# Windowed attention on Trainium2: where the band's mask for the row maxima is added

## The chip, the cores and the metric

One core of a Trainium2 chip (trn2) runs the whole program in one launch. The metric is the device time of that launch in microseconds. The kernel before takes 2782.56 us (median of three runs, 2774.63 to 2786.53).

## The reference, cut to what matters

The program is four layers of a transformer on 1024 tokens of 256 features, each layer an attention and a feed-forward part. The change concerns only the second attention (layer 1): 32 query heads and 8 key heads of 64 features, with rotary positions and a sink, a number per head that takes part in the softmax. Its core, cut:

```python
attn = jnp.einsum('bqhmd,bkhd->bhmqk', q, k) * sm_scale
...
mask = (q_pos >= k_pos) & (q_pos < k_pos + SW)
attn = jnp.where(mask, -jnp.inf, attn)
...
w = jax.nn.softmax(jnp.concatenate([attn, sink], axis=-1), axis=-1)[..., :-1]
out = jnp.einsum('bhmqk,bkhd->bqhmd', w, v).reshape(B, L, NQ * HD)
return out @ W_out
```

With SW = 64 a query leaves out itself and the 63 keys before it, and attends to all others of the 1024. In the kernel the left-out positions get -1e30 before the softmax: for a block of 128 queries they lie in a band of 192 columns of keys.

What the kernel's softmax needs before the exponentials is an upper bound of each row's scores, the row maximum. It is computed ahead, from a shorter product of queries and keys, and the mask must be in those scores too.

## The kernel before, in words

**Stages.** `layer1_attention` runs a norm, a projection (`project`, lines near 900 to 1110), `attend_window` (L1533) and an output product. Only `attend_window` changes, and what it is given in `masks_dram`.

**Batches.** `attend_window` works on 16 batches of two heads (`PER` = 2). Each has 16 tiles of scores (8 blocks of 128 keys, 2 halves of 512 queries) for each of the two heads. For batch n TensorE makes the scores (L1831, L1832, and a mask product L1834, which stays), ScalarE the exponentials (L1951), GpSimd the sums over the blocks of keys (L1754, 28 adds per batch), and TensorE the products with the values (L1847). A loop over j = 0 to 7 does two key blocks of both heads at each step.

**Maxima of the next batch, in between.** While batch n is in that loop, TensorE computes the scores for the maxima of batch n + 1, in a query-by-key orientation: 16 segments, each of one block qb of 128 queries by one half s of the keys (512), for two heads: two products of 64 rows, side by side (L1774), into a pair of banks (128 x 1024 elements). VectorE reduces each pair to its maximum in one instruction (`maxima`, L2017: 2 x 512 to 2 elements, a1h_mseg). Nine of the 16 segments are banded: the band of masked keys falls in them, 64, 128 or 192 columns of each head. Segments with their numbers, (qb, s): 0 (0,1); 1 (0,0) banded, 128 columns; 2 (4,0) banded, 64; 3 (1,1); 4 (1,0) banded, 192; 5 (4,1) banded, 128; 6 (2,1); 7 (2,0); 8 (3,1); 9 (3,0); 10 (5,0); 11 (5,1); 12 (6,0); 13 (6,1); 14 (7,0); 15 (7,1); of 7 to 15 the odd ones are banded, 192.

In the loop these go by visits: 0 and 1, then 2 (step j = 0); 3 and 4, then 5 (j = 1); 6 and 7 (j = 2); 8 and 9; 10 and 11; 12 and 13; 14 and 15 (j = 3 to 6). A visit computes the products of its segments and then, in the banded one, the mask: `mask_maxima` adds, for each 64 columns and each head, a small product (L1796) of `mk_rows` (0, 1 and -1 in bfloat16) by a triangle of -1e30, 2 to 6 products a visit. The last of them raises `a_ready`, for which VectorE waits.

**The ring of two.** The segments' products, and five other things, go in turn through two pairs of banks (`ring`, `wait_spare`), in the order in which they are issued: segments 0 to 5, D, 6, 7, T, 8 to 11, R, 12 to 15, M. M (L1807) carries the batch's row maxima over to the other orientation, D (L1859) the sums of exponentials over keys, T (L1869) their transposes, R (L1878) the inverses spread over rows. Each waits until the one two places before it has been read: D for the read of segment 4, T for that of segment 6, segment 8 for that of 7.

**VectorE's order** is written out: per step j its maxima; at j = 1 after segment 5 the low parts of the next queries (`queries_low`, L1704, two instructions, SBUF only); at j = 2 the inverse (L2055, L2058) after segment 7; at j = 4 the scaling (L2064); at j = 7 the maximum of the two segments of a block (L2030) and with the sink (L2033, both SBUF only), for which M waits, then the spread maxima (L2042), and in two of four batches the next keys (L2005 a cast, L2007 a subtraction). An engine works its instructions off in that order.

**The first batch** has no batch before it: its segments run in visits (0, 1), (3, 4), (6, 7), (8, 9) before everything else, then M, and the other eight within steps 0 and 1, and the row maxima of its second half of queries at step 2.

The lines that set what a segment costs on either engine:

```python
ps = spare(("A", n, k))
for a in range(PER):
    mm = pe.matmul(ps[:, a, :], ..., kn[HI[a], G % 2, a, half(s)], start=True, stop=lo >= hi, ...)
...
dve.tensor_reduce(mseg[:, :, qb, s], spare(("A", n, k))[:, :, :], AX.X, ALU.max).then_inc(a_read, 1)
```

Of the kernel before, what the change touches and what calls it, by code (L numbers as in the profile page):

```python
# [1532 lines left out]
def attend_window(nc, core, name, qk, k_dram, v, scale, groups, spread_dram, masks_dram, sink, before, sync, gpsimd):  # L1533
# [54 lines left out]
    with ExitStack() as ctx:  # L1588
        sem = lambda n: nc.alloc_semaphore(f"{name}_{n}")
        sb = lambda n, shape, dt=F32: ctx.enter_context(nc.sbuf_tensor(f"{name}_{n}", shape, dt))  # L1590
        c_in, kn_in, prep, keys_out = sem("c_in"), sem("kn_in"), sem("prep"), sem("keys_out")
        k0_in, k1_ones = (sem("k0_in0"), sem("k0_in1")), sem("k1_ones")
# [7 lines left out]
        mk_rows = sb("mk_rows", [P, 3 * P + 64], BF16)  # L1600
# [8 lines left out]
        mk_rows_raw = stage[:, 1, 0:3 * P + 64]  # L1609
# [6 lines left out]
        def first_in(sp, written):  # L1616
            sp.dma_start(mk_raw[:, :, :], masks_dram[:, 0:2 * MW].rearrange("p (u m) -> p u m", u=2)).then_inc(c_in, 16)
            sp.dma_start(mk_rows_raw, masks_dram[:, 2 * MW:2 * MW + 3 * P + 64]).then_inc(c_in, 16)
# [14 lines left out]
        def constants(pool, written):  # L1633
            pool.wait_ge(c_in, 64)
            pool.tensor_scalar(mk[:, :, :], mk_raw[:, :, :], 1.0, None, ALU.mult).then_inc(prep, 1)
            pool.tensor_scalar(mk_rows[:, :], mk_rows_raw, 1.0, None, ALU.mult).then_inc(prep, 1)
            pool.memset(mpos[:, :, :].bitcast(F32), 0.0).then_inc(prep, 1)
            pool.tensor_scalar(sk8[:, :], sk[:, :], 1.0 / scale, None, ALU.mult).then_inc(prep, 1)
            pool.tensor_scalar(nident[:, :], core.ident[:, :], -1.0, None, ALU.mult).then_inc(prep, 1)
# [28 lines left out]
        def spare(key):  # L1668

            return ring[use[key] % 2]  # L1670

# [87 lines left out]
        def _(pe):  # L1759
            def maxima(n, k):  # L1760
# [11 lines left out]
                lo, hi = masked(k)  # L1772
                for a in range(PER):
                    mm = pe.matmul(ps[:, a, :], QA[n % 2][HI[a], a, qb * P:(qb + 1) * P],  # L1774
                                   kn[HI[a], G % 2, a, half(s)], start=True, stop=lo >= hi, tile_position=(64 * a, 0))
                if lo >= hi:
                    mm.then_inc(a_ready, 1)

            def masked(k):

                qb, s = SEGS[k]
                return max((qb + 1) * P - BAND, s * HALF), min((qb + 1) * P, (s + 1) * HALF)

            def mask_maxima(n, k):

                qb, s = SEGS[k]
                lo, hi = masked(k)
                if lo >= hi:
                    return
                ps = spare(("A", n, k))  # L1790
                for c in range((lo - (qb + 1) * P + BAND) // 64, 3):
                    c0 = (qb + 1) * P - BAND + 64 * c
                    if c0 >= hi:
                        continue
                    for a in range(PER):
                        mm = pe.matmul(ps[:, a, c0 - s * HALF:c0 - s * HALF + 64], mk_rows[HI[a], c * P:(c + 1) * P],  # L1796
                                       mk_rows[HI[a], 3 * P:3 * P + 64], start=False, stop=c0 + 64 == hi,
                                       tile_position=(64 * a, 0))
                mm.then_inc(a_ready, 1)
# [82 lines left out]
            def visit(n, ks):  # L1882
# [3 lines left out]
                for k in ks:  # L1886
                    mask_maxima(n, k)
# [110 lines left out]
        def _(dve):  # L1998
# [15 lines left out]
            def maxima(n, k):  # L2014
                qb, s = SEGS[k]
                dve.wait_ge(a_ready, use["A", n, k] + 1)
                dve.tensor_reduce(mseg[:, :, qb, s], spare(("A", n, k))[:, :, :], AX.X, ALU.max).then_inc(a_read, 1)  # L2017
# [1382 lines left out]
def lay_out(inp):  # L3400
# [28 lines left out]
    bands = np.zeros((64, 3 * P + 64), np.float32)  # L3429
    i, j = np.arange(64), np.arange(64)[None, :]  # L3430
    for b in range(2):
        own, nxt = P * b + 64 * b, P * (b + 1) + 64 * b
        bands[i[1:], own + i[:-1]] = 1.0
        bands[i[1:], nxt + i[:-1]] = -1.0
        bands[0, nxt:nxt + 64] = 1.0
    bands[:, 3 * P:][j >= i[:, None]] = -1e30
    a["window"] = np.concatenate([m.reshape(P, 4 * P), np.concatenate([bands, bands])], 1)
# [109 lines left out]
```

## Time and profile before

| | |
|---|---|
| median of three runs | 2782.56 us |
| the profiled execution | 2789.25 us |
| its span on the chip | 2787.5 us |
| mean granted TensorE clock | 0.928 |
| TensorE busy (matmul) | 2531.3 us, 91% |
| VectorE busy | 1627.8 us, 58% |
| ScalarE busy | 1259.5 us, 45% |
| GpSimd busy | 1289.6 us, 46% |
| second attention | about 626 to 1340 us of the span |

The page of the profile calls the engines PE (matmuls), PEld (weight loads), DVE (VectorE), ACT (ScalarE), POOL (GpSimd) and SP (SyncE). A row of a timeline is: start in us from the span's start, length in us (of xN instructions merged: from the first start to the last end), engine, line, operation, output <- inputs, shapes, and in brackets how long the engine sat idle before and what released it. Matmuls overlap in their rows, so costs on TensorE are read from one start to the next. The granted clock is 1.00 at 2.4 GHz and 0.50 at 1.2 GHz.

### The profile page before, as it was taken

The numbers are of one execution on the slowest core, as the hardware profiler recorded it, in microseconds if no ns is written. First come the engines' busy times: TensorE is split into PE (matmuls) and PEld (weight loads), VectorE is DVE, ScalarE is ACT, GpSimd is POOL, SyncE is SP. The second block draws the span as 40 slices with busy tenths as digits, with TensorE's granted clock in tenths as the row PEclk, the third lists the DMA queues.
The fourth block names the chain that finished last, engine by engine and source line by source line (L and its number), as shares of the span: only waits on it lengthen the run. The fifth ranks groups of instructions, "written<-read, shape, count | busy, mean of one in ns | idle before, by whom it ended". The sixth has DMA issues, their size and how long they took to land. (4 is left out here: it accounts for less than half of the span.)

```text
span 2787.5 us, 40697 instructions
## 1 busy us (share of the span) xinstructions
PE 2531.3 (91%) x14471; PEld 1686.6 (61%) x14474; DVE 1627.8 (58%) x2168; ACT 1259.5 (45%) x2174; POOL 1289.6 (46%) x1130
## 2 busy tenths in 40 slices
PE   6887999878999999999878888789999989998798
PEld 4444777654444444444664446578888867776676
DVE  4663555577666766664436633477767745554555
ACT  4464333464555555555334552256555543333222
POOL 4100344486888888888521003254545523442243
PEclk9798999898999999999976979899999998998799
DMA  1000111121101101010000001100100001110111
GB/s 58 1 2 15 35 46 48 44 79 38 39 16 38 39 24 38 16 35 1 27 24 1 1 1 49 52 22 20 31 20 20 21 10 41 45 45 15 30 42 41
DMA packets 39709, 81.63 MB, mean 29 GB/s; under 512 B 7552, under 2 KB 21120, under 8 KB 39040
## 3 DMA queue, kind: packets, MB, share of 16 engines
q1 hardware_dynamic: 39264, 79.41, 10.2%
q8 instruction: 98, 1.61, 0.3%
q14 instruction: 59, 0.48, 0.1%
q10 hardware_dynamic: 288, 0.13, 0.0%
HBM read 59.07 MB, written 2.62 MB: 22 GB/s over the span
## 5 line engine op out<-in xcount | busy, mean ns | idle before, releaser
L2017 DVE TENSOR_REDUCE a1h_mseg<-bank 128x2 f32<-128x1024 f32 x256 | 302.7, 1222 | 187.3 <-PE bank L1774 173.4
L63 POOL TENSOR_TENSOR f_wh<-f_raw,ones_r 128x768 fp32r<-128x768 f32 (+1 forms) x74 | 111.8, 1511 | 545.6 <-PE bank L464 367.2
L1951 ACT ACTIVATE a1h_prob<-bank 128x512 f32<-128x512 f32 x366 | 206.1, 598 | 165.8 <-PE bank L1834 83.8
L1754 POOL TENSOR_TENSOR a_qk<-a_qk,a1h_prob 128x512 f32<-128x512 f32 x186 | 238.7, 1315 | 50.8 <-ACT a1h_prob L1951 50.8
L453 PE MATMUL bank<-x_norm_h,f_wh 128*128 128x512 f32 x592 | 244.2, 412 | 6.5 <-PEq L3247 2.5
L453 PE MATMUL bank<-x_norm_l,f_wh 128*128 128x512 f32 x592 | 238.7, 403 | 0.0
L453 PE MATMUL bank<-x_norm_h,f_wl 128*128 128x512 f32 x592 | 237.5, 401 | 0.0
L656 DVE SCALAR_TENSOR_TENSOR f_tf<-bank,f_bias,f_sg 128x512 f32<-128x512 f32 x148 | 111.0, 751 | 191.8 <-PE bank L453 185.4
L1832 PE MATMUL bank<-a1h_ql,a1h_k 128*128 128x512 f32 x512 | 203.2, 397 | 0.0
L544 ACT ACTIVATE f_hhi<-f_hf 128x512 fp32r<-128x512 f32 x124 | 78.3, 632 | 276.3 <-DVE f_hf L664 276.3
L1847 PE MATMUL bank<-a1h_prob,a_v 128*64 128x512 f32 x732 | 179.8, 604 | 0.0
L670 DVE TENSOR_TENSOR f_hlo<-f_hf,f_hhi 128x512 fp32r<-128x512 f32 x124 | 116.1, 938 | 82.7 <-ACT f_hhi L544 82.4
L533 ACT ACTIVATE f_sg<-bank,f_bias 128x512 f32<-128x512 f32 x148 | 101.9, 688 | 130.1 <-PE bank L453 130.1
L453 PEld LDWEIGHTS bank<-x_norm_h,f_wh 128*128 128x128 f32 x592 | 114.0, 192 | 50.8 <-issue 24.3
L453 PEld LDWEIGHTS bank<-x_norm_l,f_wh 128*128 128x128 f32 x592 | 114.1, 193 | 28.2
L364 POOL TENSOR_TENSOR f_wl<-f_raw,f_wh 128x768 fp32r<-128x768 f32 (+1 forms) x74 | 127.8, 1727 | 5.9
L453 PEld LDWEIGHTS bank<-x_norm_h,f_wl 128*128 128x128 f32 x592 | 114.7, 194 | 25.5
L464 PE MATMUL bank<-f_hhi,f_wh 128*128 128x512 f32 x296 | 118.5, 400 | 12.8 <-DVE f_hlo L670 12.8
L1831 PE MATMUL bank<-x_norm_h,a1h_kn 128*128 128x512 f32 x256 | 120.4, 470 | 4.7 <-DVE a1h_k L2012 3.4
L2871 POOL TENSOR_TENSOR l2a_rope<-l2a_rope,l2a_tab 128x512 f32<-128x512 f32 x64 | 81.2, 1276 | 88.9 <-ACT l2a_rope L2736 87.8
L1754 POOL TENSOR_TENSOR x_norm<-x_norm,a1h_prob 128x512 f32<-128x512 f32 x86 | 112.3, 1338 | 20.6 <-ACT a1h_prob L1951 20.6
L1455 ACT ACTIVATE a2h_prob<-bank 128x512 f32<-128x512 f32 (+3 forms) x192 | 83.7, 488 | 81.2 <-PE bank L1285 56.9
(595 smaller groups left out, 6337.8 us busy)
## 6 DMA issues: line engine op xcount, KB each, us to landing
f_raw<-in_l_w_dram SPq DMA_DIRECT2D x66, 385.0 KB, 3.1
a1h_st_q<-a_qk SPq DMA_DIRECT2D x128, 128.0 KB, 2.4
l2a_qkraw<-in_l2a_wqk_dram SPq DMA_DIRECT2D x32, 128.0 KB, 2.1
l2a_vraw<-in_l2a_wvg_dram SPq DMA_DIRECT2D x8, 512.0 KB, 3.8
f_raw<-in_l_w_dram SPq DMA_DIRECT2D x8, 449.0 KB, 3.3
a_qk<-l_keys SPq DMA_DIRECT2D x24, 128.0 KB, 2.8
a1p_raw<-in_l1a_w_dram SPq DMA_DIRECT2D x20, 128.0 KB, 2.1
a_qk<-in_l1a_wo_dram SPq DMA_DIRECT2D x16, 128.0 KB, 2.1
```

The lines of the kernel that those rows point to most:

```text
L63: return pool.tensor_tensor(dst, src, one.to_broadcast(list(src.shape)), ALU.mult)
L364: pool.tensor_tensor(wl[:, slot, :], raw[:, slot, 0:B], wh[:, slot, :].bitcast(F32), ALU.subtract).then_inc(w_split, 1)
L453: mm = pe.matmul(out[:, :], w[:, slot, c0:c0 + P], x, start=n == 0, stop=n == 3 * n_k - 1)
L464: mm = pe.matmul(acc[m][h][:, :], w[:, slot, c0:c0 + P], x[:, h, :], start=begin and n == 0, stop=False, skip_group_check=True)
L656: dve.scalar_tensor_tensor(tf[:, h, :], up[h][:, :], bias[:, slot, 1:2], sg[:, h, :], ALU.add, ALU.mult).then_inc(t_ready, 1)
L670: dve.tensor_tensor(hl[:, h, :], src[:, h, :], hh[:, h, :].bitcast(F32), ALU.subtract).then_inc(hl_ready, 1)
L1754: pool.tensor_tensor(out, first, slot_of[t % NP], ALU.add).then_inc(sum_done, 1)
L1831: pe.matmul(bank[:, :], kn[:, G % 2, a, keys], QA[n % 2][:, a, half(h)], start=True, stop=False)
L1832: mm = pe.matmul(bank[:, :], k1[:, a, keys], ql[:, n % 2, a, half(h)], start=False, stop=lo >= hi)
L1847: pe.matmul(core.bank[5][64 * a:64 * a + 64, :], v[:, kb, 2 * (n // 4) + a, :], slot_of[t % NP], start=kb == 0, stop=kb == TB - 1, skip_gr ...
L1951: act.activation(slot_of[t % NP], core.bank[2 + t % 3][:, :], ACT.Exp, scale=scale).then_inc(p_ready, 1)
L2017: dve.tensor_reduce(mseg[:, :, qb, s], spare(("A", n, k))[:, :, :], AX.X, ALU.max).then_inc(a_read, 1)
```

## The change

The nine banded segments of each batch get their mask from VectorE. It adds the rows of `mk` (bfloat16, the mask in query-by-key orientation, already in SBUF; its half `mk[:, 1]` was loaded before too, without a reader; L1834 reads the other) to the banded columns of both heads, in place in the bank pair: 2 x 64, 2 x 128 or 2 x 192 elements a partition, one `tensor_tensor` with one operand and the output in PSUM and the other operand in SBUF. It waits for it (`band_added`) and reduces as before. The 46 mask products per batch go, and with them `mask_maxima`, the tile `mk_rows`, its DMA and its conversion by GpSimd. `a_ready` is now raised by the segment's own product. Nothing else is moved.

```diff
--- before.py
+++ after.py
@@ -1589,6 +1589,7 @@
         sem = lambda n: nc.alloc_semaphore(f"{name}_{n}")
         sb = lambda n, shape, dt=F32: ctx.enter_context(nc.sbuf_tensor(f"{name}_{n}", shape, dt))
         c_in, kn_in, prep, keys_out = sem("c_in"), sem("kn_in"), sem("prep"), sem("keys_out")
+        band_added = sem("band_added")
         k0_in, k1_ones = (sem("k0_in0"), sem("k0_in1")), sem("k1_ones")
         q_in = [sem("q_in0"), sem("q_in1")]
         q_hi, q_lo, kn_steps, k1_act, k1_dve = sem("q_hi"), sem("q_lo"), sem("kn_steps"), sem("k1_act"), sem("k1_dve")
@@ -1597,7 +1598,6 @@
         ou_done, on_done, den_copied, r_steps, rx_done = sem("ou"), sem("on"), sem("den_copied"), sem("r_steps"), sem("rx")
         spread = sb("spread", [P, TB])
         mk = sb("mk", [P, 2, MW], BF16)
-        mk_rows = sb("mk_rows", [P, 3 * P + 64], BF16)
         nident = sb("nident", [P, P])
         mpos = sb("mpos", [P, PER, 64], F32R)
         sk = sb("sk", [P, BATCHES * PER])
@@ -1606,7 +1606,6 @@
         kn = sb("kn", [P, 2, PER, T], F32R)
         stage = sb("stage", [P, 2, HALF])
         mk_raw = stage[:, 0, 0:2 * MW].rearrange("p (u m) -> p u m", u=2)
-        mk_rows_raw = stage[:, 1, 0:3 * P + 64]
 
         def load_queries(sp, n, a):
             for r in range(4):
@@ -1615,7 +1614,6 @@
 
         def first_in(sp, written):
             sp.dma_start(mk_raw[:, :, :], masks_dram[:, 0:2 * MW].rearrange("p (u m) -> p u m", u=2)).then_inc(c_in, 16)
-            sp.dma_start(mk_rows_raw, masks_dram[:, 2 * MW:2 * MW + 3 * P + 64]).then_inc(c_in, 16)
             sp.dma_start(spread[:, :], spread_dram).then_inc(c_in, 16)
             sp.dma_start(sk[:, :], sink.partition_broadcast(P)).then_inc(c_in, 16)
             written(sp, 0)
@@ -1631,9 +1629,8 @@
                 sp.dma_start(k_dram[G], qk[:, NQ + G, :]).then_inc(keys_out, 16)
 
         def constants(pool, written):
-            pool.wait_ge(c_in, 64)
+            pool.wait_ge(c_in, 48)
             pool.tensor_scalar(mk[:, :, :], mk_raw[:, :, :], 1.0, None, ALU.mult).then_inc(prep, 1)
-            pool.tensor_scalar(mk_rows[:, :], mk_rows_raw, 1.0, None, ALU.mult).then_inc(prep, 1)
             pool.memset(mpos[:, :, :].bitcast(F32), 0.0).then_inc(prep, 1)
             pool.tensor_scalar(sk8[:, :], sk[:, :], 1.0 / scale, None, ALU.mult).then_inc(prep, 1)
             pool.tensor_scalar(nident[:, :], core.ident[:, :], -1.0, None, ALU.mult).then_inc(prep, 1)
@@ -1669,6 +1666,17 @@
 
             return ring[use[key] % 2]
 
+        def masked(k):
+
+            qb, s = SEGS[k]
+            return max((qb + 1) * P - BAND, s * HALF), min((qb + 1) * P, (s + 1) * HALF)
+
+        def bands_added(n, k):
+
+            if n == 0:
+                return sum(SEGS[x] in BANDED for x in FIRST[:FIRST.index(k) + 1])
+            return n * len(BANDED) + sum(SEGS[x] in BANDED for x in range(k + 1))
+
         def reads(n, k):
 
             return n * len(SEGS) + (k if n else FIRST.index(k)) + 1
@@ -1769,33 +1777,9 @@
                         pe.wait_ge(kn_steps, G * 4 + 4)
                 wait_spare(pe, ("A", n, k))
                 ps = spare(("A", n, k))
-                lo, hi = masked(k)
                 for a in range(PER):
                     mm = pe.matmul(ps[:, a, :], QA[n % 2][HI[a], a, qb * P:(qb + 1) * P],
-                                   kn[HI[a], G % 2, a, half(s)], start=True, stop=lo >= hi, tile_position=(64 * a, 0))
-                if lo >= hi:
-                    mm.then_inc(a_ready, 1)
-
-            def masked(k):
-
-                qb, s = SEGS[k]
-                return max((qb + 1) * P - BAND, s * HALF), min((qb + 1) * P, (s + 1) * HALF)
-
-            def mask_maxima(n, k):
-
-                qb, s = SEGS[k]
-                lo, hi = masked(k)
-                if lo >= hi:
-                    return
-                ps = spare(("A", n, k))
-                for c in range((lo - (qb + 1) * P + BAND) // 64, 3):
-                    c0 = (qb + 1) * P - BAND + 64 * c
-                    if c0 >= hi:
-                        continue
-                    for a in range(PER):
-                        mm = pe.matmul(ps[:, a, c0 - s * HALF:c0 - s * HALF + 64], mk_rows[HI[a], c * P:(c + 1) * P],
-                                       mk_rows[HI[a], 3 * P:3 * P + 64], start=False, stop=c0 + 64 == hi,
-                                       tile_position=(64 * a, 0))
+                                   kn[HI[a], G % 2, a, half(s)], start=True, stop=True, tile_position=(64 * a, 0))
                 mm.then_inc(a_ready, 1)
 
             def max_rows(n, kind="M"):
@@ -1883,8 +1867,6 @@
 
                 for k in ks:
                     maxima(n, k)
-                for k in ks:
-                    mask_maxima(n, k)
 
             for ks in HEAD:
                 visit(0, ks)
@@ -2014,6 +1996,12 @@
             def maxima(n, k):
                 qb, s = SEGS[k]
                 dve.wait_ge(a_ready, use["A", n, k] + 1)
+                lo, hi = masked(k)
+                if lo < hi:
+                    part = spare(("A", n, k))[:, :, lo - s * HALF:hi - s * HALF]
+                    band = mk[:, 1, lo - (qb - 1) * P:hi - (qb - 1) * P].unsqueeze(1)
+                    dve.tensor_tensor(part, part, band.to_broadcast([P, PER, hi - lo]), ALU.add).then_inc(band_added, 1)
+                    dve.wait_ge(band_added, bands_added(n, k))
                 dve.tensor_reduce(mseg[:, :, qb, s], spare(("A", n, k))[:, :, :], AX.X, ALU.max).then_inc(a_read, 1)
 
             def blocks(n, kind):
@@ -3426,15 +3414,7 @@
     c2 = np.arange(2 * P)[None, :]
     m[:, 0][(c2 >= k) & (c2 < k + 64)] = -1e30
     m[:, 1][(P + k - c2 >= 0) & (P + k - c2 < 64)] = -1e30
-    bands = np.zeros((64, 3 * P + 64), np.float32)
-    i, j = np.arange(64), np.arange(64)[None, :]
-    for b in range(2):
-        own, nxt = P * b + 64 * b, P * (b + 1) + 64 * b
-        bands[i[1:], own + i[:-1]] = 1.0
-        bands[i[1:], nxt + i[:-1]] = -1.0
-        bands[0, nxt:nxt + 64] = 1.0
-    bands[:, 3 * P:][j >= i[:, None]] = -1e30
-    a["window"] = np.concatenate([m.reshape(P, 4 * P), np.concatenate([bands, bands])], 1)
+    a["window"] = m.reshape(P, 4 * P)
     pos = np.arange(T, dtype=np.float32)
 
     r = np.arange(P)
```

## Rows read from the trace of the kernel before

**Rows 1.** Busy time by stretch: start:end, length, then busy us of each engine, clock, DMA.
```profile
640.00:660.00 20.00, 16.62 (x80) 8.27 (x79) 12.01 (x12) 6.35 (x12) 8.39 (x7) 0.75 0.09 20
820.00:860.00 40.00, 37.32 (x224) 17.84 (x222) 25.76 (x23) 20.81 (x35) 30.85 (x25) 1.00 0.17 40
```

**Rows 2.** Timeline of TensorE: two visits, one of two segments, one of one (start, length).
```profile
929.16 0.74 PE L1774 MATMUL bank<-a1h_kn,x_norm_l 64*128 64x512 f32 x4
929.74 0.26 PE L1796 MATMUL bank<-a1h_mk_rows 64*128 64x64 bf16 x6
929.93 0.65 PE L1847 MATMUL bank<-a1h_prob,a_v 128*64 128x512 f32 x2
...
964.07 0.50 PE L1774 MATMUL bank<-a1h_kn,x_norm_h 64*128 64x512 f32 x2
964.41 0.23 PE L1796 MATMUL bank<-a1h_mk_rows 64*128 64x64 bf16 x4
964.57 1.06 PE L1859 MATMUL bank<-a_qk,ones_r 128*32 128x512 f32 x8
```

**Rows 3.** Single lines, VectorE: duration in ns, least/median/most.
```profile
L1089 DVE TENSOR_TENSOR bank<-bank,a1p_tab x40: 689/699/700, 541.9 to 609.5; 128x512 f32<-128x512 f32 x40
...
L2064 DVE TENSOR_TENSOR a_qk<-a_qk,bank x16: 1220/1222/1223, 719.3 to 1347.4; 128x1024 f32<-128x1024 f32 x16
```

**Rows 4.** Timeline, first stretch, in two batches; last row: waits (us, times, longest).
```profile
917.20 0.73 PE L1774 MATMUL bank<-a1h_kn,x_norm_l 64*128 64x512 f32 x4
917.74 2.36 DVE L2017 TENSOR_REDUCE a1h_mseg<-bank 128x2 f32<-128x1024 f32 x2 [1.70 <-PE bank L1774]
920.34 0.62 PE L1859 MATMUL bank<-a_qk,ones_r 128*32 128x512 f32 x1
921.71 3.59 DVE L1704 TENSOR_TENSOR a1h_ql<-a1h_st_q,x_norm_l 64x1024 fp32r<-64x1024 f32 x2
922.92 7.21 POOL L1754 TENSOR_TENSOR a_qk<-a_qk,a1h_prob 128x512 f32<-128x512 f32 x5 [1.58 <-ACT a1h_prob L1951]
926.62 0.66 PE L1869 MATMUL bank<-ident,a1h_dsum 128*128 128x128 f32 x4 [0.42 <-DVE a1h_mseg L2017]
...
961.43 0.73 PE L1774 MATMUL bank<-a1h_kn,x_norm_h 64*128 64x512 f32 x4
965.83 2.46 DVE L1704 TENSOR_TENSOR a1h_ql<-a1h_st_q,x_norm_h 64x1024 fp32r<-64x1024 f32 x2
970.36 0.66 PE L1869 MATMUL bank<-ident,a1h_dsum 128*128 128x128 f32 x4
...
PE bank L1869 <- DVE a1h_mseg L2017: 2.0, 5, 0.4
```

**Rows 5.** Timeline, second stretch: GpSimd, VectorE and TensorE around the row maxima.
```profile
939.01 9.93 POOL L1754 TENSOR_TENSOR a_qk<-a_qk,a1h_prob 128x512 f32<-128x512 f32 x8 [2.14 <-ACT a1h_prob L1951]
947.74 1.23 DVE L2030 TENSOR_TENSOR a1h_mrow<-a1h_mseg 128x16 f32<-128x16 f32 x1
949.00 0.18 DVE L2033 TENSOR_TENSOR a1h_mpos<-a1h_mrow,a1h_sk 128x16 fp32r<-128x16 f32 x1
949.13 2.51 POOL L1754 TENSOR_TENSOR a_qk<-a_qk,a1h_prob 128x512 f32<-128x512 f32 x2 [0.20 <-ACT a1h_prob L1951]
949.96 0.44 PE L1807 MATMUL bank<-a1h_nident,a1h_mpos 128*64 128x128 f32 x4
```

**Rows 6.** Single lines, VectorE: one subtraction behind a cast, beside GpSimd and without.
```profile
L2007 DVE TENSOR_TENSOR a1h_kn<-a_qk,a1h_kn x6: 2189/2194/2197, 735.1 to 1128.0; 64x1024 fp32r<-64x1024 f32 x6
...
L1647 DVE TENSOR_TENSOR a1h_kn<-x_norm,a1h_kn x2: 1218/1220/1223, 612.3 to 614.6; 64x1024 fp32r<-64x1024 f32 x2
```

**Rows 7.** Timeline, the start of the second attention.
```profile
626.40 9.53 DVE L2017 TENSOR_REDUCE a1h_mseg<-bank 128x2 f32<-128x1024 f32 x8 [2.06 <-PE bank L1774]
658.27 0.17 DVE L2030 TENSOR_TENSOR a1h_mrow<-a1h_mseg 128x8 f32<-128x8 f32 x1
659.07 1.28 POOL L1754 TENSOR_TENSOR a_qk<-a_qk,a1h_prob 128x512 f32<-128x512 f32 x1 [5.55 <-ACT a1h_prob L1951]
```

## The prediction

> **What bounds the kernel now.** I read the busy time by stretch first. In the second attention (about 626 to 1340 us) TensorE is busy 37 of 40 us or more at the full granted clock, the stretch shown being the least busy of the steady ones, VectorE about 26; only the first 20 us or so differ, with the clock at 0.75 [rows 1]. So TensorE is the bound on average, and a mask taken off it looks like a gain. The page and the waits do not say whether VectorE, which gets the work, is late at the few places where TensorE asks it for a result. For that I read one batch of two heads in order of time (a batch is 43 to 45 us; a batch's maxima are taken in nine visits, each of which ends with one masked segment).
>
> **The products removed.** A batch has 23 blocks of 64 masked columns, for two heads: 46 products, 736 in all, and all go. Their busy times overlap, so I take starts. A visit of two segments has its first mask product 0.58 us after its first product, a visit of one 0.34: a pair of products costs 0.24, and the step into the masks 0.10. The six masks and the step out of them take 0.19 (929.74 to 929.93), four take 0.16 [rows 2]. Per visit that is 0.29 with six and 0.26 with four (a few have two). Part of it stays, since the next work sits in another tile form anyway: between nothing and the 0.10 seen on the way in. I take 0.07, nearer the row. A visit gives 0.22 (six masks) or about 0.20 (four or two), bounds 0.16 to 0.29; nine visits, 1.9 us a batch.
> The Trainium skill (TensorEngine Tiling (Array Packing), Tiling Modes) states that changing the tiling mode drains TensorE; the masks use the same form as the products before them, so by that rule the drain stays and only the lower end of the saving comes, 0.03 less a visit, and the sum would be about 2 us higher. No row shows a step out without masks.
>
> **The adds.** No row shows this add, but one is almost it: VectorE's multiply in place on a bank, 512 elements, 0.689 to 0.700 us, of which I take 0.695. One of 1,024 with a bank and a tile in SBUF takes 1.222 [rows 3]. The slope is 1.03 ns an element, so 384 elements cost 0.56, 256 cost 0.43, 128 cost 0.30. The reduction waits for the add: 0.03 us more, as between the two small operations at 947.74 and 949.00 [rows 5]. Per batch 6 x 0.59 + 2 x 0.46 + 0.33 = 4.8 us of VectorE. Bounds: 0.30 an add (half the price; then the first collision below goes too) and 0.70 (the 512-element row whole). I take the line through the two rows, since both are of this form.
>
> **Stretch 1, from the visit of segments 3 and 4 to the transposes of the sums (L1869).** Before, it takes 9.42 us (917.20 to 926.62) in five batches, where the transposes wait for VectorE 0.4 us, and 8.93 (961.43 to 970.36) in the nine others [rows 4]. They need the bank that segment 6 was read from; VectorE reads it after segments 3, 4, 5 and the two halves of the queries' low part (L1704). After: first reduction 0.54 behind the visit, 1.18, add 0.59, 1.18, add 0.46, 1.22, then L1704. The sums over keys (L1859) need segment 4's bank, which is read at 0.54 + 1.18 + 0.59 + 1.22 + 0.07 = 3.60, where TensorE would have been there at 3.14 - 0.42 = 2.72: a stall of 0.88. GpSimd's next add comes 2.58 behind L1859 (920.34 to 922.92), at 6.18. L1704's first half then runs from 5.20 to 6.42, so GpSimd waits in it and comes before its second half.
> That collision is real in the trace: in the five long batches GpSimd starts (922.92) just as the first half ends, and the pair takes 3.59 in place of 2.46. And a GpSimd that waits gets in between two VectorE instructions 0.03 apart: the subtraction behind the cast takes 2.19 in all six cases, 1.22 where it meets no GpSimd add [rows 6]. So: 5.20 + 1.22 + 1.25 + 1.25 + 1.22 + 0.07 = 10.21. That is 0.79 more than before in five batches, 1.28 in nine.
>
> **Stretch 2, from there to the row maxima's product (L1807).** 23.34 us (926.62 to 949.96). Four visits give 0.88. But VectorE's maximum of two segments (L2030) asks at 947.74, while GpSimd's eighth add in a run is on (939.01 to 948.94), and ends with it at 948.97; GpSimd's ninth comes at 949.13 only, so L2033 slips in [rows 5]. After, L2030 asks 0.37 later (0.59 for the last add, less 0.22 for the visit before), still inside the eighth add, and ends as before. The ninth is ready 0.44 earlier, 948.69, so GpSimd is waiting when L2030 ends and goes first: L2033 ends at about 950.4 and L1807 starts at 950.5, 0.54 late rather than 0.44 early. The two visits further up still give 0.44. Net +0.10.
>
> **Stretch 3, to the next visit of segments 3 and 4.** Two visits: -0.37. The adds there (0.46 + 0.33) end before anyone asks.
>
> **The start.** The first eight reductions run without a gap, 9.53 us, and scores wait for them: four adds, 2.2 us. The first batch's other eight go through the two banks in two groups, with TensorE behind them: about 0.6 a group. Then the row maxima of its second half: L2030 asks at 658.27, just ahead of GpSimd's run at 659.07 [rows 7]. After, four more adds (2.3) stand before it, against 1.2 by which GpSimd's run moves, so it and L2033 land in the run and wait as in stretch 2: about 1.9 more for TensorE. Total +5.3; what the visits of this batch save is in it, since TensorE stands waiting there.
>
> **The rest.** One of SyncE's DMAs for constants and one GpSimd conversion go, both in the projection before; nothing that TensorE or VectorE waits for there comes from them, so I take nothing, with a gain of a microsecond or two as the other end. SyncE's loads of the next queries wait for L1704, so they start up to 2 us later; ScalarE asks for them half a batch later, so they stay covered.
>
> **Sum.** Five batches at +0.79 + 0.10 - 0.37 = 0.52, nine at 1.01: 11.7. With the start 17.0 us. The profiled execution took 2789.25 (span 2787.5), which gives 2806; it stands 6.7 above the median of 2782.56, and against that the forecast is 2800. What this measurement can tell from no change is about 0.5%, 14 us, so the forecast lies just outside.
>
> **Rivals.**
> First, faster: VectorE's adds are covered, both collisions stay away. It is decided at 6.42, the end of L1704's first half: if GpSimd asks later (now 0.24 before), or if a waiting GpSimd loses to the next VectorE instruction. Then stretch 1 is TensorE's, 8.93 - 0.64 + 0.88 = 9.17, stretch 2 gives 0.88: nine batches at -1.01, five at -1.50, and the start at 3.4: -13, 2769. For it: VectorE has a third of its time free. Against it: six cases of six. The Trainium skill (SBUF — State Buffer, A bandwidth-pool intuition that's wrong) has a blocked GpSimd start about 115 ns after VectorE's end; by it VectorE's next instruction would come first, and the time would be this one. Chance 0.09.
> Second, one collision of the two: without the second, a batch gives back 0.98 us and the start 1.9: 17.0 - 15.6 = +1.4; without the first, nine batches at -0.03, five at -0.52, and the start's 5.3: +2.4. Time 2784 to 2785, chance 0.28. What speaks for it is how thin the margins are: 0.24 us for the first, 0.28 for the second (948.69 against 948.97).
> Third, dearer: the adds cost 0.70, or TensorE's new stalls of about 1 us bring the granted clock down, as in the start, where it was 0.75. Against it: all steady stretches show 1.00, that with the most idle time (2.7 of 40 us) too [rows 1]. The adds alone make the way to the transposes 0.14 + 0.27 longer in fourteen batches, and the start 1.1: 7 us, 2807; the clock more, 2812 and up. Chance 0.08.
> The forecast itself has 0.55, of which a fifth falls under 14 us (a saving near 0.29).
>
> **How the numbers follow.** Faster by over 0.5%: 0.09. Within: 0.28 + 0.11 = 0.39. Slower: 0.44 + 0.08 = 0.52. The range leaves out the lower part of the first rival and the clock: 2774 to 2811. The forecast's own range is 2793 to 2807 (saving per visit 0.16 to 0.30, adds 0.50 to 0.65).
>
> **What would show it.** Right: L1859 with a wait for VectorE near 0.9 us, L1869 near 1 us, in nearly all batches; L1704's second halves at 2.4 us; L2033 at 1.4 and not 0.18; the adds at 0.56; a batch of 44 to 45.5 us; the granted clock 1.00. Wrong: L1704 pairs at 2.46 and L2033 at 0.18 (first rival), adds far from 0.56, visits whose next work starts less than 0.5 or more than 0.6 us behind their first product (six masks).

## The result, and the profile after

| | before | after |
|---|---|---|
| median of nine runs each | 2786.68 us | 2797.70 us |
| ratio, 95% interval | | 1.0043 [1.0029, 1.0057] |
| span of the profiled execution | 2787.5 us | 2800.6 us |
| TensorE busy, instructions | 2531.3 us, 14471 | 2518.0 us, 13735 |
| VectorE busy, instructions | 1627.8 us, 2168 | 1713.4 us, 2312 |

The kernel became 11 us slower, where 17 had been forecast. That is a little less than the 0.5% (14 us) that the prediction set as the line of what can be told, so it falls in the class "within", which had 0.39, and not in "slower", which had 0.52; with nine runs a side the interval lies above 1 all the same. The forecast time of 2800 us lies 2.3 us from the measured 2797.70, closer than the change itself (17 for 11), only because the median of the kernel before is 2786.68 over nine runs and was 2782.56 over three: that part is luck.

Where the time went is read more finely in the trace than in the run times. I call **stage** the time from the second attention's first product of maxima to its last sums over keys (L1859, now L1843). It is 715.1 us before (625.85 to 1340.94) and 728.4 after (628.70 to 1357.12): +13.3. The rest of the span is 2072.4 and 2072.2. Over all twelve kernels of this study that rest lies between 2065.8 and 2076.0, so a single span, or a median of few runs, scatters by some us with nothing that the edits touch; a batch of the stage repeats within 0.05 us in most cases. The stage has three parts in each batch, the prediction's stretches: from the visit of segments 3 and 4 to the transposes of the sums (L1869, now L1853); from there to the row maxima's product (L1807, now L1791); from there to the next visit.

The first stretch in the trace of after, a batch at the same point of the stage as in [rows 4], TensorE, VectorE and GpSimd merged (start, length, engine, line):
```profile
927.39 0.73 PE L1781 MATMUL bank<-a1h_kn,x_norm_l 64*128 64x512 f32 x4
927.93 1.23 DVE L2005 TENSOR_REDUCE a1h_mseg<-bank 128x2 f32<-128x1024 f32 x1 [0.71 <-PE bank L1781]
928.05 1.08 PE L1831 MATMUL bank<-a1h_prob,a_v 128*64 128x512 f32 x4
929.08 0.56 DVE L2003 TENSOR_TENSOR bank<-bank,a1h_mk 128x384 f32<-128x384 f32 x1
929.66 1.23 DVE L2005 TENSOR_REDUCE a1h_mseg<-bank 128x2 f32<-128x1024 f32 x1
...
930.80 0.42 DVE L2003 TENSOR_TENSOR bank<-bank,a1h_mk 128x256 f32<-128x256 f32 x1
930.95 0.62 PE L1843 MATMUL bank<-a_qk,ones_r 128*32 128x512 f32 x1 [0.53 <-DVE a1h_mseg L2005]
931.26 1.23 DVE L2005 TENSOR_REDUCE a1h_mseg<-bank 128x2 f32<-128x1024 f32 x1
932.40 3.50 DVE L1712 TENSOR_TENSOR a1h_ql<-a1h_st_q,x_norm_l 64x1024 fp32r<-64x1024 f32 x2
933.53 10.93 POOL L1762 TENSOR_TENSOR a_qk<-a_qk,a1h_prob 128x512 f32<-128x512 f32 x8 [1.97 <-ACT a1h_prob L1933]
935.93 1.23 DVE L2005 TENSOR_REDUCE a1h_mseg<-bank 128x2 f32<-128x1024 f32 x1
937.21 0.66 PE L1853 MATMUL bank<-ident,a1h_dsum 128*128 128x128 f32 x4 [0.52 <-DVE a1h_mseg L2005]
```
What to see: the add costs 0.56 us and the reduction follows some 0.03 later; the sums over keys now wait 0.53 for VectorE; GpSimd's add starts as the first half of the low part ends and stands before the second (the pair takes 3.50); the transposes wait 0.52. From 927.39 to 937.21 it is 9.82 us, and 9.81 to 9.83 in all fourteen batches, where it was 8.9 in nine and 9.4 in five.

The low part's line in the after trace, the two halves of every second batch (ns, least/median/most):
```profile
L1712 DVE TENSOR_TENSOR a1h_ql<-a1h_st_q,x_norm_h x14: 1206/1727/2267, 711.5 to 1244.2; 64x1024 fp32r<-64x1024 f32 x14
```
The halves are 1.21 and 2.27 us; with every pair at 3.49 or 3.50, that is one of each in every batch.

The end of the second stretch in the same batch:
```profile
949.41 12.43 POOL L1762 TENSOR_TENSOR a_qk<-a_qk,a1h_prob 128x512 f32<-128x512 f32 x10 [2.05 <-ACT a1h_prob L1933]
956.76 0.56 DVE L2003 TENSOR_TENSOR bank<-bank,a1h_mk 128x384 f32<-128x384 f32 x1
957.35 1.23 DVE L2005 TENSOR_REDUCE a1h_mseg<-bank 128x2 f32<-128x1024 f32 x1
958.62 0.79 DVE L2018 TENSOR_TENSOR a1h_mrow<-a1h_mseg 128x16 f32<-128x16 f32 x1
959.43 1.20 DVE L2021 TENSOR_TENSOR a1h_mpos<-a1h_mrow,a1h_sk 128x16 fp32r<-128x16 f32 x1
960.78 0.44 PE L1791 MATMUL bank<-a1h_nident,a1h_mpos 128*64 128x128 f32 x4 [0.60 <-DVE a1h_mpos L2021]
```
GpSimd's run no longer has a gap behind its eighth add (ten in a row, against eight and two in [rows 5]), so the second small step waits for an add too: 1.20 and not 0.18. The stretch is 23.57, against 23.34.

TensorE's waits in the after trace, 690 to 1330 us (total us, times, longest). Before, the first and third were not there and the second was 2.0, 5 times [rows 4]:
```profile
PE bank L1791 <- DVE a1h_mpos L2021: 8.9, 15, 0.6
PE bank L1853 <- DVE a1h_mseg L2005: 7.2, 14, 0.5
PE bank L1843 <- DVE a1h_mseg L2005: 7.2, 14, 0.5
```

The stretches of [rows 1] in the trace of after: the clock of the steady part stays 1.00, VectorE is at 30.5 of 40 us where it was about 26.
```profile
640.00:660.00 20.00, 12.99 (x44) 6.65 (x44) 11.51 (x16) 7.12 (x10) 7.48 (x6) 0.67 0.00 1
820.00:860.00 40.00, 36.87 (x179) 16.66 (x178) 30.46 (x32) 21.32 (x37) 32.77 (x26) 1.00 0.17 40
```

What a visit gained, TensorE in the after trace, a visit of two segments and one of one:
```profile
972.12 0.74 PE L1781 MATMUL bank<-a1h_kn,x_norm_h 64*128 64x512 f32 x4
972.78 1.08 PE L1831 MATMUL bank<-a1h_stage,a_v 128*64 128x512 f32 x4
...
969.19 0.50 PE L1781 MATMUL bank<-a1h_kn,x_norm_h 64*128 64x512 f32 x2
969.62 0.50 PE L1815 MATMUL bank<-x_norm_l,a1h_kn 128*128 128x512 f32 x1
```
The next work starts 0.66 us behind the first product, against 0.77 in [rows 2]. So six masks with the step into them were worth 0.11 us, not 0.22. The visit of one segment shown here is that of segment 2, which had two masks: 0.43, where it is 0.48 in the trace before. Four masks in segment 5's visit, the one in [rows 2], were worth 0.09: e1, where nothing waits there, has 0.42 in place of 0.50 to 0.51. Four in segments 0 and 1 gave 0.08. Over nine visits that is 0.9 us a batch.

### The profile page after: what moved, and what is told of

Same layout as the page of the kernel before. It is cut to its first block and busy times, and to the rows that moved or that the text cites. A ratio compares the mean times of both kernels' runs of the same rounds, so it can differ in the third digit from the quotient of the medians.

```text
span 2800.6 us, 39367 instructions
## 1 busy us (share of the span) xinstructions
PE 2518.0 (90%) x13735; PEld 1669.2 (60%) x13738; DVE 1713.4 (61%) x2312; ACT 1259.5 (45%) x2174; POOL 1287.8 (46%) x1129
## 5 line engine op out<-in xcount | busy, mean ns | idle before, releaser
L2005 DVE TENSOR_REDUCE a1h_mseg<-bank 128x2 f32<-128x1024 f32 x256 | 313.2, 1226 | 133.9 <-PE bank L1781 128.4
L364 POOL TENSOR_TENSOR f_wl<-f_raw,f_wh 128x768 fp32r<-128x768 f32 (+1 forms) x74 | 128.0, 1730 | 5.9
L1815 PE MATMUL bank<-x_norm_l,a1h_kn 128*128 128x512 f32 x256 | 118.7, 464 | 0.8
## 6 DMA issues: line engine op xcount, KB each, us to landing
a1h_st_q<-a_qk SPq DMA_DIRECT2D x128, 128.0 KB, 2.4
l2a_qkraw<-in_l2a_wqk_dram SPq DMA_DIRECT2D x32, 128.0 KB, 2.3
a_qk<-l_keys SPq DMA_DIRECT2D x24, 128.0 KB, 2.6
a1p_raw<-in_l1a_w_dram SPq DMA_DIRECT2D x20, 128.0 KB, 2.0
a_qk<-in_l1a_wo_dram SPq DMA_DIRECT2D x16, 128.0 KB, 2.0
```

The costliest lines, as they stand in the source:

```text
L364: pool.tensor_tensor(wl[:, slot, :], raw[:, slot, 0:B], wh[:, slot, :].bitcast(F32), ALU.subtract).then_inc(w_split, 1)
L1815: pe.matmul(bank[:, :], kn[:, G % 2, a, keys], QA[n % 2][:, a, half(h)], start=True, stop=False)
```

## The experiments

All parts are in us and from one profiled execution each. The code shown is part of the difference to the kernel before, for e1 and e5 of that to the kernel after. Start: first product to the first visit of segments 3 and 4; 13: the thirteen batches from there, with their sums of the three stretches; the ratio is to the kernel before on the same chip.

| kernel | ratio, 95% | stage | start | 13 | to T | T to M | M on |
|---|---|---|---|---|---|---|---|
| before | | 715.1 | 73.4 | 567.3 | 118.5 | 303.7 | 145.2 |
| after | 1.0043 [1.0029, 1.0057] | 728.4 | 77.8 | 575.2 | 127.7 | 306.1 | 141.4 |
| e1 neither | 0.9981 [0.9968, 0.9995] | 708.8 | 72.6 | 561.9 | 115.8 | 304.8 | 141.4 |
| e2 both | 1.0056 [1.0038, 1.0075] | 731.3 | 80.2 | 575.9 | 127.3 | 303.6 | 145.0 |
| e3 after, low part moved | 1.0053 [1.0034, 1.0072] | 729.8 | 80.6 | 574.5 | 120.0 | 303.6 | 150.9 |
| e4 before, low part moved | 1.0013 [1.0000, 1.0026] | 720.9 | 74.7 | 571.6 | 116.1 | 306.5 | 149.0 |
| e5 after, one step | 1.0016 [0.9998, 1.0034] | 720.7 | 77.3 | 568.6 | 127.7 | 297.4 | 143.5 |
| e6 products for segments 4, 5 | 1.0006 [0.9987, 1.0026] | 714.3 | 76.7 | 563.2 | 114.8 | 306.8 | 141.6 |
| e7 products in the first batch | 1.0060 [1.0037, 1.0084] | 724.8 | 73.9 | 575.3 | 127.2 | 306.5 | 141.7 |
| e8 before, adds for 4, 5 | 1.0025 [1.0010, 1.0040] | 725.1 | 73.2 | 576.6 | 128.0 | 303.7 | 145.0 |
| e9 combined | 0.9954 [0.9939, 0.9969] | 705.2 | 74.5 | 556.8 | 115.0 | 298.2 | 143.7 |
| e10 before, one step | 1.0002 [0.9986, 1.0019] | 715.1 | 73.4 | 567.3 | 118.5 | 303.7 | 145.1 |

**e1, neither products nor adds.** What the products alone are worth. It is the kernel after without the add and its wait, so the maxima hold no mask at all.
```diff
-                lo, hi = masked(k)
-                if lo < hi:
...
-                    dve.tensor_tensor(part, part, band.to_broadcast([P, PER, hi - lo]), ALU.add).then_inc(band_added, 1)
```


> The changed kernel without its adds: no mask in the maxima at all (that part of the computation is left out: the band's -1e30 in the maxima). It shows what the products alone are worth. Theory (the after trace: a visit's next work starts 0.66 us behind its first product, before 0.77, so a visit is worth 0.11 and not 0.22; the rest of the change is what VectorE's adds cost): nine visits give 1.0 us a batch; the way to the transposes may take back 0.3 of it where GpSimd now meets the low part of the queries. 6 to 14 us below before, 2773 to 2780, ratio 0.995 to 0.998; VectorE busy as before. Rival (the products are worth the forecast's 1.9 us a batch and the adds cost that much more): 27 us below before, 2760, ratio 0.990. Rival (the loss does not come from the adds at all, but from the products' absence, the clock or the order): within 3 us of after, 2795 and up.

Measured: 2779.76 against 2783.83 us, ratio 0.9981, stage 6.3 below before. The low end of the theory was 6; the first rival's 27 is out, and so is the second's time near that of after. The visits give 0.11 each, but the stretch from transposes to row maxima is 23.54 in place of 23.36 in eleven of thirteen batches, although its four visits are 0.44 shorter. In the other two of the thirteen it is 22.9; there the first of VectorE's two steps meets no GpSimd add (0.18 us). The two steps in the e1 trace, 690 to 1400 us (ns), and one instance:
```profile
L2015 DVE TENSOR_TENSOR a1h_mpos<-a1h_mrow,a1h_sk x15: 1153/1202/1303, 690.8 to 1295.4; 128x16 fp32r<-128x16 f32 x15
...
948.81 1.34 DVE L2012 TENSOR_TENSOR a1h_mrow<-a1h_mseg 128x16 f32<-128x16 f32 x1
950.18 1.23 DVE L2015 TENSOR_TENSOR a1h_mpos<-a1h_mrow,a1h_sk 128x16 fp32r<-128x16 f32 x1
```
So the second collision needs no adds. Taking the products away is enough: TensorE's scores, and GpSimd's adds behind them, come earlier, and the gap in GpSimd's run closes.

**e2, products and adds both.** What the adds alone cost.
```diff
                 dve.wait_ge(a_ready, use["A", n, k] + 1)
+                lo, hi = masked(k)
+                if lo < hi:
...
+                    dve.tensor_tensor(part, part, band.to_broadcast([P, PER, hi - lo]), ALU.add).then_inc(band_added, 1)
```


> The kernel before with its mask products kept and VectorE's adds put in as well (the mask is added twice, which changes no weight). It shows what the adds alone cost. Theory: the way to the transposes is VectorE's, 9.82 us as in the after trace, 0.41 more than before in five batches and 0.89 more in nine; the row maxima come about 0.6 late; the start costs 4.4 + 1: 5 x 1.0 + 9 x 1.5 + 5.4 = 24 us above before, 2810, that is 11 to 13 above after. Rival (a visit's products are worth the forecast's 0.22): 0.22 x 9 x 14 = 27 above after, 2825. Rival (VectorE's adds are what costs, and the products' time is hidden under them): equal to after within 3 us, 2798.

Measured: 2803.31 us, ratio 1.0056; stage 16.2 above before, where 24 was expected, and 2.9 above after, where 11 to 13 was: a miss on both. What came, at its edge, is the last rival, by which the products' time is hidden under the adds (within 3 us of after). The second small step, 690 to 1400 us, is not held up here:
```profile
L2046 DVE TENSOR_TENSOR a1h_mpos<-a1h_mrow,a1h_sk x15: 174/176/178, 699.1 to 1318.7; 128x16 fp32r<-128x16 f32 x15
```
So with the products kept, the adds cost nothing in the second stretch (303.6): TensorE isn't waiting for VectorE there. They cost it in the first stretch (+8.8) and at the start (+6.8). With the adds in, dropping the products is worth 2.9 us in the whole stage, and the thirteen batches only 0.7: the first stretch is VectorE's anyway, the second becomes 2.5 us longer and the third 3.6 shorter.

**e3 and e4, the low part moved.** L1712 taken out of the first stretch.
```diff
-                    if n + 1 < BATCHES and j == 1:
-                        for a in range(PER):
-                            queries_low(dve, n + 1, a)
...
+                    if n + 1 < BATCHES and j in (3, 4):
+                        queries_low(dve, n + 1, j - 3)
```


> The changed kernel with the low part of the next queries taken out of VectorE's way to the transposes: its first half behind the maxima of the fourth pair of tiles, its second behind the scaling in the fifth, where VectorE has 1.2 to 1.7 us free. Theory (VectorE's order with the low part in it, held up by a GpSimd add, sets when the transposes start): their wait for VectorE goes, 9.82 becomes 9.2 to 9.3 (the sums over keys still wait 0.5), 14 x 0.55 = 8 us below after, 2790, ratio to before 1.001. Rival (the time lost is in the adds before the sums over keys and before the row maxima, and what is won here is waited for there): within 2 us of after, 2796 to 2800.

> The same move in the kernel before, as the control. Theory: only the five batches in which the transposes wait 0.4 us gain, 5 x 0.48 = 2.4 us below before, 2784, ratio 0.999. Rival (the move is worth the same in both kernels, so it says nothing of the change): 8 us below before, 2778, ratio 0.997.

Measured: e3 2801.92, e4 2788.56 us; no gain in either, against the theory of both. The theory's own step came: to the transposes 9.23 in all batches of e3 (9.2 to 9.3 expected), and e4's five long ones went. But it is paid back elsewhere, as e3's rival had it. In e3 against after the first stretch gives 7.7 us and the second 2.5, the third takes 9.5, and the start is 2.8 longer. In e4 against before the first gives 2.4, the third takes 3.9 and the second 2.8 (L2033 meets GpSimd now, 1.21 us in the median). The largest part of e3's loss, 2.5 us each, is in the three batches where the next visit waits for new keys. There, in e3, behind the row maxima:
```profile
792.15 1.64 DVE L1987 CAST a1h_kn<-a_qk 128x1024 fp32r<-128x1024 f32 x1
793.23 0.60 ACT L1933 ACTIVATE a_qk<-bank 128x512 f32<-128x512 f32 x1 [0.32 <-POOL x_norm L1762]
793.82 2.19 DVE L1989 TENSOR_TENSOR a1h_kn<-a_qk,a1h_kn 64x1024 fp32r<-64x1024 f32 x1
796.11 0.73 PE L1781 MATMUL bank<-a1h_kn,x_norm_h 64*128 64x512 f32 x4 [1.82 <-issue]
796.77 3.54 PE L1831 MATMUL bank<-a1h_prob,a_v 128*64 128x512 f32 x8
```
In after the same subtraction takes 1.22 (all six), the visit waits 0.88 and the eight products of values take 1.94. Moved work didn't change what the order costs, only where VectorE and GpSimd meet. That the slower values come from weights held up behind GpSimd's late sums is how I read the ScalarE row; no run took that apart.

**e5, the row maxima in one step.** The sink's floor is copied into its slot earlier, at step j = 5.
```diff
-                dve.tensor_tensor(mrow[:, :, b], mseg[:, :, b, 0], mseg[:, :, b, 1], ALU.max).then_inc(m_steps, 1)
...
-                dve.tensor_tensor(mpos[:, :, b], mrow[:, :, b], low, ALU.max).then_inc(m_steps, 1)
+                dve.wait_ge(low_in, n + 1)
+                dve.tensor_reduce(mpos[:, :, b], mseg[:, :, b, :], AX.X, ALU.max).then_inc(m_steps, 2)
...
+                dve.tensor_copy(mseg[:, :, :, NH], low).then_inc(low_in, 1)
```


> The changed kernel with the row maxima's two small VectorE steps (maximum of two segments, maximum with the sink's floor; 0.79 + 1.20 us in the after trace, each held up by a GpSimd add) made one: a reduction over three slots, the third filled with the floor earlier. Stage time below means from the second attention's first product of maxima to its last sums over keys in the trace: 715.1 before, 728.4 after. Theory (the second step's wait for GpSimd holds the row maxima's product 0.6 us in every batch): from transposes to row maxima 22.9 in place of 23.54, 14 x 0.6 + 0.6 at the start = 9 us less: stage 719, 2789, ratio to before 1.001. Rival (the visits after it only meet GpSimd elsewhere and wait there): stage 725 or more, 2795 and up.

Measured: 2788.24 us, ratio 1.0016, stage 720.7. From transposes to row maxima 22.87 to 22.90, as the theory had it; 2 us of the 9 went in the third stretch of three batches, 12.2 there in place of 11.56: TensorE's scores wait longer for VectorE's cast of new keys (1.75 us, in after 1.09). The one step in the e5 trace, with GpSimd's run over it (ns):
```profile
944.43 12.41 POOL L1762 TENSOR_TENSOR a_qk<-a_qk,a1h_prob 128x512 f32<-128x512 f32 x10 [2.03 <-ACT a1h_prob L1933]
953.70 0.20 DVE L2019 TENSOR_REDUCE a1h_mpos<-a1h_mseg 128x16 fp32r<-128x48 f32 x1
955.13 0.44 PE L1791 MATMUL bank<-a1h_nident,a1h_mpos 128*64 128x128 f32 x4
...
L2019 DVE TENSOR_REDUCE a1h_mpos<-a1h_mseg x17: 178/202/204, 639.0 to 1304.1; 128x16 fp32r<-128x48 f32 x15, 128x8 fp32r<-128x24 f32 x2
```

**e6, products kept for segments 4 and 5; e7, for the first batch.** Both have a function choose who masks; shown for e6, in e7 the condition is `n > 0`.
```diff
+        def on_vector(n, k):
+
+            return SEGS[k] in BANDED and (k not in (4, 5))
...
+                if on_vector(n, k):
+                    lo = hi
...
-                if lo >= hi:
+                if lo >= hi or on_vector(n, k):
                     return
```


> The changed kernel with the mask products kept for the two masked segments between the visit of segments 3 and 4 and the transposes' bank (segments 4 and 5), in all batches; the other seven have VectorE's add. Theory (these two adds, with the GpSimd add that gets between the halves of the low part, cost 0.41 us in five batches and 0.89 in nine): the visit to the transposes is 8.9 to 9.4 again, 10 us below after, one add less at the start: stage 718 (before 715.1, after 728.4), 2787, ratio to before 1.0005. Rival (the order has slack there and the other seven adds are what costs): within 3 us of after, 2796.

> The changed kernel with the first batch's maxima masked by products as before and all later ones by VectorE. Theory (the start costs 4.4 us in the trace, since TensorE stands behind VectorE's reductions there): stage 724, from the first product to the first visit of segments 3 and 4 73.4 in place of 77.8; 2793, ratio to before 1.0025. Rival (what is won at the start is waited for at the first row maxima of batch 1): stage 727 to 728, 2797.

Measured: e6 2786.72 us, ratio 1.0006, stage 714.3 (718 expected): two adds fewer per batch give 14 us back, 4 more than expected. The stretch is 8.83 to 8.85 in all fourteen batches, where the kernel before has five of 9.4. Here no GpSimd add gets between the halves of the low part: all 28 take 1.21 to 1.22 us. And it is below before's 8.93, since the visit before the transposes keeps its saving:
```profile
921.69 0.74 PE L1792 MATMUL bank<-a1h_kn,x_norm_l 64*128 64x512 f32 x4
922.46 1.08 PE L1860 MATMUL bank<-a1h_prob,a_v 128*64 128x512 f32 x4
924.83 0.62 PE L1872 MATMUL bank<-a_qk,ones_r 128*32 128x512 f32 x1
930.52 0.66 PE L1882 MATMUL bank<-ident,a1h_dsum 128*128 128x128 f32 x4
```
e7: stage 724.8 (724 expected), start 73.9 for 77.8, as the theory had it; the run time, 2800.75 us over a range of 26 us, does not show it. By the times alone e7 is inconclusive.

**e8, only the two adds of segments 4 and 5, products elsewhere.**
```diff
+            return SEGS[k] in BANDED and (n > 0 and k in (4, 5))
```

> The kernel before with only two of the nine adds, those of segments 4 and 5 in the batches behind the first; products elsewhere. Theory: these two alone make the way to the transposes 9.82 in every batch and nothing else changes (23.36 from there to the row maxima): 5 x 0.41 + 9 x 0.89 = 10 us above before: stage 725, 2794 to 2796, ratio 1.0036. Rival (the loss needs the other adds and the row maxima's step that waits for GpSimd): stage 718, within 3 us of before.

Measured: stage 725.1, as expected to 0.1; 2791.57 us, ratio 1.0025, so 7.7 us by the times (2794 to 2796 expected). Its stretches are before's but for the first, 9.8 to 9.95 in thirteen of fourteen. TensorE's waits in it, 690 to 1350 us:
```profile
PE bank L1872 <- DVE a1h_mseg L2036: 8.1, 14, 0.7
PE bank L1882 <- DVE a1h_mseg L2036: 5.2, 13, 0.4
```
Two adds of nine make three quarters of the change's +13.3, with all the products still in.

**e9, e6 and e7 and the one step together; e10, e5's edit in the kernel before.**
```diff
+            return SEGS[k] in BANDED and (n > 0 and k not in (4, 5))
...
+                dve.tensor_reduce(mpos[:, :, b], mseg[:, :, b, :], AX.X, ALU.max).then_inc(m_steps, 2)
```

> What the runs so far point to, in one kernel: mask products for the first batch and for segments 4 and 5, VectorE's adds for the other seven masked segments of every later batch, and the row maxima in one VectorE step. Theory (the four places add up): start 73.4 as before, visit to transposes 8.83, from there to the row maxima 22.9, then 10.4 to 12.2: 13 batches in 554 us (before 567.3), stage 702 (before 715.1), 13 below before: 2771, ratio 0.995. Rival (a gain in one place is waited for in the next, as with the low part moved): stage 710 or more, ratio 0.998 and up.

> The control: the kernel before with the one-step row maxima alone, all mask products kept. Theory (there the second step meets no GpSimd add, 0.18 us, and TensorE is not waiting for it): 23.36 from transposes to row maxima stays, stage 713 to 716, ratio 0.999 to 1.001. Rival (the one step is a gain of its own of 0.6 us a batch, whoever masks): stage 707, ratio 0.997.

Measured: e9 2770.06 us against 2783.53, ratio 0.9954 [0.9939, 0.9969], faster than both kernels; stage 705.2, 9.9 below before, where 13 was expected: the start is 1.1 longer, and three third stretches are 12.25, as in e5 and not 11.56 as in after, which is 2 us more. e10: stage 715.07 against 715.09; the one step is worth nothing until the second step has something to wait for.

## Why the prediction was right in sign and 6 us too high

By its own steps, in the trace (+13.3 in the stage, 17.0 forecast; 11.0 in the medians).

**The saving per visit failed**, and below its own bounds: 0.22 (0.16 to 0.29) forecast for six masks, 0.11 measured, 0.9 us a batch and not 1.9. The step was "Part of it stays, since the next work sits in another tile form anyway: between nothing and the 0.10 seen on the way in". What stays is 0.18: a further pair of products would start at 0.48 (twice 0.24), the next work comes at 0.66. The step out of the products is dearer than the step from products to masks, which no row before could show. The rule on tiling modes of the Trainium skill (TensorEngine Tiling (Array Packing), Tiling Modes) pointed the right way, to the lower end; the trace agrees with its direction and lies 0.08 below the 0.19 a visit that I had worked out beside it. That the change of form is what the 0.18 pays for is not shown: in no run is the next work in the same form. If TensorE set the time everywhere, this error would have put it 14 us higher (1.0 a batch). Most of that is hidden, since VectorE sets the first stretch and the start: with the adds in, all the products are worth 2.9 us (e2 against after).

**The adds were right**: 0.56, 0.42 and 0.29 us, forecast 0.56, 0.43, 0.30.

**Stretch 1 was right in its mechanism, both waits and the GpSimd add between the halves in all fourteen batches, and 0.39 too long**: 9.82, forecast 10.21. The waits are 0.53 and 0.52, forecast 0.9 and near 1. I spaced the reductions at 1.18 and 1.22; start to start it is 1.14, and L1712 starts 5.01 behind the visit, not 5.20; the held-up pair took 3.53, not 1.22 + 1.25 + 1.25. Over 14 batches it is 5 x 0.41 + 9 x 0.89 = 10.1, forecast 15.5. e8 shows it by itself.

**Stretch 2 was right but for the share of the adds**: +0.19 a batch, +0.10 forecast; L2021 at 1.20, forecast 1.4. I had both causes, the later L2030 and the earlier ninth add; e1 and e2 show that the earlier GpSimd alone does it. So the saving of TensorE brings this wait about, and takes the saving with it: four visits give 0.44, the stretch is 0.19 longer.

**Stretch 3**: -0.13 to -0.17 in ten batches (two visits of 0.11 and less), -0.7 to -0.9 in three, where scores wait for VectorE's cast of new keys, 1.4 us in all in place of 3.4: the cast takes 1.09 us (L1994), before 1.72 (L2012), by my reading since it meets less of a GpSimd add. Together -3.7 in thirteen; forecast -0.37 each, -4.8.

**The start**: +4.4, forecast +5.3. The forecast wait of 1.9 didn't come: GpSimd's run starts at 665.27, just as the two steps are nearly done (0.17 each). The step that failed here is how far GpSimd moves: counted from the first product, the two steps come 3.8 us later and GpSimd's run 3.4, where 2.3 and 1.2 had been put. The rest of the start cost 4.4 and not 3.4. TensorE is at the lower clock for longer (0.67 from 640 to 660 us, where it was 0.75), but no run takes the clock apart from the adds, and e2's start is the longer one, 80.2, at 0.80 in the same window. e7 confirms the size: 73.9 with products in the first batch. The two steps, beside GpSimd's run:
```profile
664.96 0.17 DVE L2018 TENSOR_TENSOR a1h_mrow<-a1h_mseg 128x8 f32<-128x8 f32 x1
665.17 0.17 DVE L2021 TENSOR_TENSOR a1h_mpos<-a1h_mrow,a1h_sk 128x8 fp32r<-128x8 f32 x1
665.27 4.95 POOL L1762 TENSOR_TENSOR a_qk<-a_qk,a1h_prob 128x512 f32<-128x512 f32 x4 [6.70 <-ACT a1h_prob L1933]
```

**The rest** at nothing: 2072.4 and 2072.2 us. Of the **rivals**, the first needed a waiting GpSimd to lose to the next VectorE instruction; it won in all fourteen batches. By the prediction's reading of the Trainium skill (SBUF — State Buffer, A bandwidth-pool intuition that's wrong), a blocked GpSimd starting about 115 ns after VectorE's end, VectorE's next would have come first. That section measures DMA descriptors that GpSimd can't write and says nothing of who comes first, so the order was an inference, and the trace doesn't agree with it: the first half of the low part ends at 933.61, and the GpSimd add is recorded from 933.53. The second needed one collision to stay away, and neither did; the third needed adds of 0.70 or a lower clock, and they took 0.56 and the clock stayed at 1.00 from 680 to 1330 us. Of the **signs** that the prediction named, the adds, the low part's second halves (2.27 for 2.4), the second small step (L2021, before L2033; 1.20 for 1.4), the batch (44.2 us in the mean) and the clock came as forecast or near it. One sign of being wrong came too: a visit's next work starts more than 0.6 us behind its first product, at 0.66.

Against the forecast, stretch 1 is 5.4 us lower, the start 0.9 lower, stretch 2 1.2 higher and stretch 3 1.5: 17.0 - 3.6 = 13.4. The saving was too high and the loss in stretch 1 too, so the number is nearer than its terms; that these errors offset each other is luck.

## What to carry to other kernels

An average of busy time does not say who sets the time where engines ask each other for a result: VectorE, busy 26 of 40 us, had little or no slack at the two places of the first stretch, and two adds of 0.58 and 0.46 us there cost 10 us in all, more than the products of all nine visits were worth (6.3, e1). Before moving work from a full engine to one with time to spare, follow the receiving engine through one period instruction by instruction, and move only what lands in its gaps; e9 does that for the first stretch, the row maxima and the first batch, and beats both kernels. Where VectorE and GpSimd share work, making TensorE faster or moving an instruction shifts who meets whom, so each place has to be looked at again after each edit.

## What was not expected of the hardware

A small VectorE operation with both inputs in SBUF takes 0.17 us alone and 1.20 us when it meets a GpSimd add, and a copy of 16 numbers a partition took 0.7 to 1.9 us in e9; a reduction over 48 numbers in SBUF took at most 0.204 us in all fifteen cases of e5, each in the midst of a GpSimd add. The Trainium skill (SBUF — State Buffer, Who interferes with whom) says that a reduction never contends with GpSimd on this chip, and that an operation with two SBUF inputs contends with a GpSimd instruction that reads SBUF, as the adds here do; the trace agrees with both.

Six small products cost TensorE only 0.11 us where work in another tile form follows anyway: behind the last pair of products the next work starts 0.18 later than a further pair would, and 0.29 later with six masks between.
